# Attention output projection: one fp32 product becomes three 16-bit products, with W_o split in the prologue and the attention result split at its eviction

## What is computed

```python
x = _layernorm(x + attention(x), axis=-1)
x = _layernorm(x + experts(x), axis=-1)
# in attention, per head, with w, k, v, r projected from the normalised x:
state = (1.0 - wt)[..., None] * state + kt[..., None] * vt[..., None, :]
y = jnp.einsum('bhs,bhst->bht', rt, state)
return (y @ Wo, state_f)
```

## Time and profile before

| what | value |
|---|---|
| median of 3 runs | 868.62 us (864.68 to 868.86) |
| profiled execution | 866.74 us |
| its span, first to last instruction | 864.9 us |
| TensorE matmul, busy | 736.8 us (85%), 6073 records |
| VectorE busy | 489.1 us (57%) |
| ScalarE busy | 344.0 us (40%) |
| GpSimd busy | 328.2 us (38%) |
| L349, the output projection, busy | 59.9 us in 128 records (two records for each of 64 fp32 products) |
| mean granted TensorE clock | 0.934 of 2.4 GHz |
| the attention block ends at about | 498 us of the span |

### The profile page before, as it was taken

One profiled execution on the slowest core, in us unless ns is written; L12 is line 12 of the kernel. 1 busy time (PEld: TensorE's weight loads), 2 busy tenths in 40 slices (PEclk: granted clock), 3 DMA queues, 4 the chain that ended last, 5 costly groups with the idle time before them and its releaser, 6 DMA issues. The chain is left out here.

```text
span 864.9 us, 18399 instructions
## 1 busy us (share of the span) xinstructions
PE 736.8 (85%) x6073; PEld 522.8 (60%) x6074; DVE 489.1 (57%) x992; ACT 344.0 (40%) x718; POOL 328.2 (38%) x355
## 2 busy tenths in 40 slices
PE   5889999998999989999879752999999999999400
PEld 3657786967878768777646431656666666666200
DVE  4656867666676666767656466343434444343285
ACT  5455645455454454454564220222222222222154
POOL 0345544443345424554333004233333333433262
PEclk9999999998999989999989965999999999999855
DMA  8515335440454314543243094155455457222394
GB/s 341 219 58 170 110 106 147 147 136 30 132 147 147 114 36 147 147 143 102 72 125 99 0 352 181 39 182 178 154 203 186 175 185 275 86 85 86 121 341 157
DMA packets 38866, 126.73 MB, mean 147 GB/s; under 512 B 3984, under 2 KB 4368, under 8 KB 36496
## 3 DMA queue, kind: packets, MB, share of 16 engines
q1 hardware_dynamic: 31920, 103.31, 35.5%
q0 software_dynamic: 6880, 22.55, 7.7%
HBM read 81.02 MB, written 44.83 MB: 146 GB/s over the span
## 5 line engine op out<-in xcount | busy, mean ns | idle before, releaser
L831 DVE COPY_PREDICATED ST<-msk,pS 128x256 f32<-128x256 uint8 x224 | 121.1, 569 | 101.4 <-issue 67.2
L577 POOL TENSOR_TENSOR piece_parts<-piece,piece_parts 128x1024 f16<-128x1024 f32 x48 | 104.3, 2172 | 113.7 <-ACT piece_parts L523 113.7
L571 POOL TENSOR_TENSOR L<-L,AM 128x256 f32<-128x256 f32 x96 | 71.1, 741 | 118.8 <-ACT L L515 107.7
L1236 PE MATMUL pH<-ring,xgh 128*128 x344 | 103.8, 302 | 2.4 <-DVE xgl L1468 2.4
L1237 PE MATMUL pH<-ring,xgh 128*128 x344 | 103.7, 302 | 0.0
L1238 PE MATMUL pH<-ring,xgl 128*128 x344 | 103.7, 302 | 0.0
L299 PE MATMUL pS<-L 64*128 64x64 f32 x1536 | 98.4, 274 | 4.8 <-issue 4.8
L1553 POOL DMA_INDIRECT y_scratch<-ysb,sidx x43 | 42.9, 998 | 146.5 <-DVE ysb L1479 146.5
L299 PEld LDWEIGHTS pS<-L 64*128 64x128 f32 x1536 | 92.9, 191 | 5.1 <-issue 5.1
L1464 DVE TENSOR_TENSOR hid<-pH,sil 128x320 f32<-128x320 f32 x43 | 21.1, 492 | 114.6 <-ACT sil L1317 114.6
L555 DVE TENSOR_TENSOR L<-L,AM 128x256 f32<-128x256 f32 x96 | 70.6, 736 | 16.1 <-ACT L L502 9.9
(11 more groups left out here) (206 smaller groups left out, 1623.6 us busy)
## 6 DMA issues: line engine op xcount, KB each, us to landing
piece<-in_w_experts SPq DMA_DIRECT2D x48, 512.0 KB, 5.5
w_split_scratch<-piece_parts SPq DMA_DIRECT2D x48, 512.0 KB, 3.9
ring<-w_split_scratch SPq DMA_DIRECT2D x12, 2048.0 KB, 8.5
yin<-y_scratch SPq DMA_DIRECT2D x16, 512.0 KB, 6.1
x_scratch<-X SPq DMA_DIRECT2D x1, 4096.0 KB, 14.1
out_x<-X SPq DMA_DIRECT2D x8, 512.0 KB, 2.8
X<-in_x SPq DMA_DIRECT2D x1, 3072.0 KB, 22.8
X<-in_x SPq DMA_DIRECT2D x2, 512.0 KB, 7.2
```

What stands on the lines that cost most here:

```text
L571: g.tensor_tensor(next_kept(k, lv, 0), kept(key, k, lv, 0), by, ALU.mult).then_inc(k_dec, 1)
L577: g.tensor_tensor(piece_parts[buf][:, 1, :], piece[buf][:, :], piece_parts[buf][:, 0, :], ALU.subtract).then_inc(piece_lo, 1)
L831: v.copy_predicated(out[:, :, :, 0 if lv == 0 else 1, :], msk[:, lv, :, :].rearrange(shape, m=m), pS[:, :, lv * S:(lv + 1) * S].rearrange( ...
L1236: pe.matmul(p[:, 0, 0:F], xgh[par][:, k, :], wh, start=(k == 0), stop=False)
```

## The change

`w_o` in fp32 gives way to `wo_h` and `wo_l` in fp16, and `yT` to `yTh` and `yTl`. W_o is loaded in two halves into `val[1]` and `rec[1]`, buffers of pair 1 that are not in use yet; ScalarE casts each half (two instructions of 128x1024) just ahead of its chunk 0, and GpSimd subtracts (two of 128x1024) between its levels of chunk 0 and of chunk 1. ScalarE's evictions into those two buffers (jobs 6 and 8 of pair 1) wait for that. ScalarE's copy of `pY` now writes `yTh` in fp16, and VectorE gets a new instruction, `low_y(n - 1)`, which stands first in chunk n and waits for that copy. TensorE's `attend_out` has 12 products where it had 4, and it and `read_state`, which overwrites `pY`, also wait for `low_y`.

```diff
-        w_o = sb("w_o", [P, KT, C])
+        wo_h = sb("wo_h", [P, KT, C], F16)
+        wo_l = sb("wo_l", [P, KT, C], F16)
...
-        yT = sb("yT", [P, KT, P])
+        yTh = sb("yTh", [P, KT, P], F16)
+        yTl = sb("yTl", [P, KT, P], F16)
...
+        wo_stage = [val[1][:, :, :], rec[1][:, :, :]]
...
-            sp.dma_start(w_o[:, :, :], wo).then_inc(w_in[5], 16)
+            for i in range(2):
+                sp.dma_start(wo_stage[i], wo[:, 2 * i:2 * i + 2, :]).then_inc(w_in[5], 16)
...
                 pe.wait_ge(y_out, n + 1)
+                pe.wait_ge(y_low, n + 1)
...
             def attend_out(n):
+                pe.wait_ge(wo_lo, 2)
                 pe.wait_ge(y_out, n + 2)
+                pe.wait_ge(y_low, n + 2)
...
                 for g in range(KT):
-                    i = pe.matmul(pM[:, 0, :], yT[:, g, :], w_o[:, g, :], start=(g == 0), stop=(g == KT - 1))
+                    pe.matmul(pM[:, 0, :], yTh[:, g, :], wo_h[:, g, :], start=(g == 0), stop=False)
+                    pe.matmul(pM[:, 0, :], yTh[:, g, :], wo_l[:, g, :], start=False, stop=False)
+                    i = pe.matmul(pM[:, 0, :], yTl[:, g, :], wo_h[:, g, :], start=False, stop=(g == KT - 1))
...
-                a.copy(yT[:, :, :], pY[:, 0, :].rearrange("p (g t) -> p g t", g=KT)).then_inc(y_out, 1)
+                a.copy(yTh[:, :, :], pY[:, 0, :].rearrange("p (g t) -> p g t", g=KT)).then_inc(y_out, 1)
...
             a.wait_ge(stat1, 9)
+            for i in range(2):
+                a.wait_ge(w_in[5], 32)
+                a.copy(wo_h[:, 2 * i:2 * i + 2, :], wo_stage[i]).then_inc(wo_hi, 1)
             chunk(0, 0, 0, 0, (1, 1, SECOND))
...
+                if not isinstance(n, int) or n:
+                    low_y(n - 1)
                 if k % 2 and nxt is not None:
                     dve_decays(v, n + 1, nxt, in_pair(k + 1)[0])
                 level(0)
...
+            def low_y(n):
+
+                v.wait_ge(y_out, n + 2)
+                v.tensor_tensor(yTl[:, :, :], pY[:, 0, :].rearrange("p (g t) -> p g t", g=KT), yTh[:, :, :], ALU.subtract).then_inc(y_low, 1)
...
-            for n in range(2):
-                pool_chunk(g, n, n, 0)
+            pool_chunk(g, 0, 0, 0)
+            for i in range(2):
+                g.wait_ge(wo_hi, i + 1)
+                g.tensor_tensor(wo_l[:, 2 * i:2 * i + 2, :], wo_stage[i], wo_h[:, 2 * i:2 * i + 2, :], ALU.subtract).then_inc(wo_lo, 1)
+            pool_chunk(g, 1, 1, 0)
```

More of the change, by code:

```diff
@@ L166, in attention @@
         y_out = sem("y_out")
+        y_low = sem("y_low")
+        wo_hi = sem("wo_hi")
+        wo_lo = sem("wo_lo")
         m_full = sem("m_full")
@@ L424, in _ @@
             pe.wait_ge(setup_done, 1)
-            pe.wait_ge(w_in[5], 16)
             chunk(0, 0, (1, 1, SECOND))
@@ L593, in take @@
                 a.wait_ge(a_full, order(q, m) + 1)
+                if isinstance(q, int) and q == 1 and (m == 6 or m == 8):
+                    a.wait_ge(wo_lo, 2)
                 if n is not None and m == 4:
@@ L894, in _ @@
             v.sem_inc(state_new, 1)
+            v.sem_inc(y_low, 1)
             v.sem_inc(x1_ready, 1)
@@ L942, in _ @@
                 chunk(n, n, None if n == NT - 1 else NPAIR - 1)
+            low_y(NT - 1)
             add_out(NT - 1)
```

## The result

| | before | after |
|---|---|---|
| median | 868.68 us (864.68 to 873.7, 15 runs) | 878.39 us (871.27 to 882.22, 15 runs) |
| ratio to before, 95% interval | | 1.0103 [1.0079, 1.0128] |
| profiled execution, its span | 866.74 us, 864.9 us | 881.45 us, 879.6 us |
| mean granted TensorE clock there | 0.934 | 0.915 |

The change costs 9.7 us between the medians, 1.0% by the ratio of the runs. The forecast was 867.4 us and no change; the result is 0.4 us above the range, where rival (b), the falling clock, had put it (877.8).

What follows compares the result with a forecast made beforehand. TensorE was taken to bound even chunks, VectorE's chain to xl the odd ones. Terms +2.9 + 1.8 - 5.3 + 0.8 - 0.8 - 0.6 = -1.2 us gave 867.4 us, no change; range 861 to 878.

Steps and rivals of the forecast that it cites:

- rival (b): TensorE's pauses in chunks 1, 3, 7, 11 drop its clock: 10.4 us more, 877.8 us; chance 0.2.
- The products: Projection in even chunks 2 to 12: 12 fp16 products take 2.64 us against 3.53, six chunks give -5.3 us.
- The wait in odd chunks: Chunks 3, 7, 11: subtraction ahead of nine products makes mask 0.86 us late, xl 0.54; 0.6 each, +1.8 us.
- rival (c): GpSimd collides with VectorE's decays in their new place, chunks 1, 3, 7, 11, 13: +2.8 us, 871.4; chance 0.18.
- Prologue and chunk 1: W_o's split delays yT by 1.9 us to 90.5; mask at 95.6, xl 2.9 us late: chunk 1 +2.9 us.
- a sign of being wrong: A wait for kbT or the keys in a chunk that had none before would show the forecast wrong.
- The clock at 1.00 outside the jumps back: TensorE's clock was to stay at 1.00 everywhere except behind the loop's jumps back.
- Chunk 15: Attention block's last chunk: its projection gains 0.89 us less 0.1 for a mask nearly due, -0.8 us.
- Chunk 14: TensorE waits at its end for a piece's DMA through ScalarE, so its 0.89 us gain is lost: 0.
- Chunk 13: Odd chunk without xl: the late mask pushes two levels and add_out(12), 0.86 us arriving nearly whole: +0.8 us.
- The last projection: Block's end: starts 0.6 us later, but 12 short products lose less in the same clock dip: net -0.6 us.
- Chunks 5 and 9: Behind the jump back TensorE itself stalls 2.50 us and more, so VectorE's new wait costs 0.

Runs made afterwards that it cites:

- e1: Changed kernel with the low-half subtraction and its wait placed behind the decays and level 0 instead of ahead: 874.89 us, ratio 1.0048.
- e2: Kernel before, fp32 projection kept, plus only the subtraction at each chunk's head and its waits, result unused: 877.56 us, ratio 1.0068.
- e4: Changed kernel with the split of W_o moved ahead of chunk 0's work on ScalarE and GpSimd: 876.77 us, ratio 1.0077.
- e9b: Kernel before, fp32 projection kept, with extra VectorE subtractions that make xl late in the loop's odd chunks: 886.12 us, ratio 1.0186.
- e10: Changed kernel with late subtraction, early W_o split and moved z job, plus eight throw-away products at chunk 14's end: 858.05 us, ratio 0.9848.
- e7: Kernel before, fp32 projection kept, with odd chunks' z job moved behind the first apply_values and second scores: 867.37 us, ratio 0.9967.
- e5: Changed kernel with both the subtraction behind the decays and level 0 and the early W_o split: 869.04 us, ratio 0.9985.
- e6: Changed kernel with late subtraction and early W_o split, plus odd chunks' z job behind first apply_values and second scores: 861.50 us, ratio 0.9894.
- e3: Changed kernel with the 12 projection products issued twice in odd chunks 1 to 11, same values: 876.75 us, ratio 1.0058.
- e11: The kernel of e10 plus fourteen throw-away products in chunk 13's wait for the first normalised x: 857.95 us, ratio 0.9858.

## Why the prediction was wrong, step by step

- **The products: right.** 12 in 2.64 us were forecast; four groups at 0.65 us are 2.60. An even chunk is 24.15 us for 24.1, six of them -5.1 us for -5.3, and nothing in them came late.
- **The wait in odd chunks: the mechanism right, the size short.** The mask was forecast 0.86 us late and was 0.80. The term of 0.6 per chunk came out as 1.0, because I carried the lateness through the mask at its old duration. The nine products ahead of the mask took 3.41 us (146.12 to 149.53) for 3.42 forecast, though a key level of GpSimd lay beside them, so rival (c) didn't come where I had put it. The mask's pause grew by 0.36 us and `xl` by 0.17 beside GpSimd's levels, which the move had brought under them. If that reading holds, it is a small form of rival (c), in the mask and not in the decays. My idle time of 2.1 us was also short of my own terms (0.80 + 0.89 + 0.6 = 2.3); 2.55 was measured. e1 takes the 1.0 away, e2 brings it back without the products.
- **Prologue and chunk 1: the lateness right, a wait missed.** `yT` was forecast at 90.5 and came at 91.09, the subtraction at 91.1 and 91.72, the mask at 95.6 and 96.29. Chunk 0 itself was 0.68 us later, which I had put at 0, and which is the whole of these misses; the prologue's first z job is already 0.69 us later (39.52 for 38.83), and it lies between 38.83 and 40.16 in the 13 profiles. I had no wait for `kbT` in chunk 1, and had named one as a sign of being wrong: it is there, 2.49 us, since ScalarE's copy ahead of `kbT` waits for the late level 0 (2.98 us, until 96.40). TensorE then waits for `xl` all the same, so it is a second pause rather than time of its own. Chunk 1 lasted 4.52 us longer instead of 2.9; 1.7 of that is a clock of 0.50 from 102.8 to 106.2 in the z job (102.50 to 106.88, 4.38 us; in chunk 7 it is 2.71), and e4, without the lateness, has chunk 1 at 27.90.
- **"The clock at 1.00 outside the jumps back": this step failed.** No term of the sum has the clock in it, and over the runs the change spends 20.7 us more at 0.50, worth up to 10.3 us, while the forecast was missed by 11.0. Chunks 1 and 3 fell in this profile: 1.7 and 1.6 us. Rival (b) had the cause, TensorE standing still, and e9b shows it alone. But (b) priced it from one row, 2.6 us a fall, and let it happen in all of four chunks, 10.4 us. It happens in a third of the chunks with a pause of 2.55 us, and costs 1.3 to 1.7 us. Its total was nearly right by a sum that was not.
- **Chunk 15: this term was the largest miss,** -0.8 forecast, +5.68 measured. The wait for `logitT` at its head is the one that I had put at the end of chunk 14, and into which I let chunk 14's 0.89 us go. It grew from 1.25 to 1.90 us, and I priced that in time and not in clock: the clock fell for 13.70 us, all of it TensorE's work (13.49 busy). The -0.8 for chunk 15's own projection, which stands behind that wait, was too much as well. In e1, the one unfilled kernel with 16-bit products that kept the clock there, the chunk is 22.10 us for 21.66 before: 0.80 more for a wait of 2.05 us, and 0.36 less behind it (19.39 for 19.75), where TensorE now also waits 0.50 us for the mask. e10 gives 4.7 us back by filling that wait. Chunk 14 (0 forecast, +1.41) has 5.7 us at 0.50, 1.0 before: the stretch behind chunk 13's pauses runs from 437.3 to 450.9 and chunk 14 begins at 445.21; before it ran from 429.4 to 439.6, and the chunk began at 438.60. e2, e7 and e9b, all with fp32 products, have a stretch of 13.7 us there too, so its length doesn't follow from the products alone. Chunk 13 itself was right, +0.51 for +0.8.
- **The last projection: -0.6 forecast, +0.56 measured.** "12 short products lose less in the same dip" supposed the same dip. Now all twelve ran at 0.50, at a pitch of 0.43 us, 5.1 us in all for 5.37 before, as in the rows below.
- **Chunks 5 and 9: 0 forecast, +0.74 and +0.60.** The stretch at 0.50 behind the jump back is 10.2 us after, and 6.8 before. e1, e2, e4 and e5 have the longer stretch in at least one of the two turns, e7 too at the second, so that it doesn't follow from the change alone. Why it is longer stays open.

```profile
504.06 0.58 PE L359 MATMUL pM<-wo_h,yTh 128*128 128x512 f16 x1 [3.62 <-DVE yTl L899]
504.44 0.63 PE L360 MATMUL pM<-wo_l,yTh 128*128 128x512 f16 x1
504.87 0.63 PE L361 MATMUL pM<-wo_h,yTl 128*128 128x512 f16 x1
```

The chances carried the same error. (b) had 0.2, since one stretch of the prologue with little work had kept its clock. That stretch holds one pause of 2.51 us, so it was the right place to look, but it was one execution: with the same pause there the clock fell in five profiles of 13. One row can't tell "never" from "in one case of three", and the falls wanted a term of their own, a chance times a price for each pause that grew.

## What to carry to other kernels

When a change shortens TensorE's work ahead of a wait that another engine ends, the time turns into pause and not into gain, and the pause can take the clock down behind it: list the waits behind each shortened piece, look in several executions for how often pauses of about that length are followed by 0.50, and put that chance times the price of a fall into the sum. First move work into such a wait (here the z job, 7.5 us); where none can be moved, products that are thrown away can pay: 1.9 us of them gave 4.7 us back in chunk 15, where TensorE is the bound behind the pause; 3.2 us of them gave nothing in chunk 13, where a pause of 5.30 us follows. A subtraction that needs another engine's result shouldn't stand at the head of an in-order list: behind the decays it costs nothing in the loop.

## What the runs showed of the hardware

- A pause of 2.55 to 2.71 us of TensorE was followed by a stretch at 1.2 GHz in 4 chunks of 12 (chunks 3, 7 and 11), the same program falling in chunk 3 in one execution and in chunk 11 in another. Pauses of 1.64 to 1.74 us in the same place: 0 of 9. In the prologue a pause of 2.51 to 2.78 us was followed by one in 5 profiles of 13.
- In chunk 15 pauses of 1.79 to 2.12 us were followed by a fall in 6 of 7, and one of 1.54 us in e2 was too; in chunk 1 a fall came behind a pause of 0.81 us (e6). So the pause's length alone doesn't decide; what else does wasn't tested.
- Time at 1.2 GHz was worth less than half of its length: 12.6 us less of it came with 4.7 us with chunk 15 filled (e10 against e6), 10.5 us less with 1.6 us between the medians and about 4 by the ratios with the odd chunks filled (e3 against the changed kernel).
- Of 26 jumps back of the loop, 24 were followed by a stretch of 6.8 or 10.2 us at 1.2 GHz; the two chunks without one took 27.54 and 28.91 us, 4.6 and 4.5 us less than in the kernel to compare with (e11 against e10, e3 against the changed kernel, a profile each).
- Five decays of 1.86 us became 4.39 us in e1 beside a GpSimd subtraction of 2.14 us and two key levels; one key level alone beside them left them at 1.86 us.
